# Self-attention's row maxima turned by VectorE and two DMAs instead of by TensorE and ScalarE, from the fourth batch on

## What is computed

```python
q = qkv[:, :, 0].transpose(0, 2, 1, 3)
k = qkv[:, :, 1].transpose(0, 2, 1, 3)
v = qkv[:, :, 2].transpose(0, 2, 1, 3)
attn = jnp.einsum('bhnd,bhsd->bhns', q, k) * SCALE
attn = jax.nn.softmax(attn, axis=-1)
o = jnp.einsum('bhns,bhsd->bhnd', attn, v)
```

## Time and profile before

| | us |
|---|---|
| median of 3 runs | 2573.73 |
| lowest and highest | 2573.45, 2574.57 |
| the profiled execution | 2577.71 |
| its span, first instruction to last | 2575.9 |
| what lies around the span | 1.8 |

### The profile page before, as it was taken

How to read it: one execution, slowest core, us unless ns; L and a number is a source line. 1 busy time by engine, 2 the same in 40 slices (tenths; PEclk the granted TensorE clock), 3 DMA queues, 4 the chain that set the end, 5 groups by cost and what they waited for, 6 DMA issues and landing times.

```text
span 2575.9 us, 66165 instructions
## 1 busy us (share of the span) xinstructions
PE 2479.3 (96%) x27466; PEld 1848.3 (72%) x27466; DVE 1858.5 (72%) x3532; ACT 1274.0 (49%) x1810; POOL 467.2 (18%) x510
## 2 busy tenths in 40 slices
PE   5779999999999999999999999999999999999998
PEld 3557777777777777777777777777777777777767
DVE  4767777777777777777777767777677677776752
ACT  1345544555555555555455554554555545445443
POOL 0111211212111211111121211211212212112121
PEclk7889999999999999999999999999999999999999
DMA  5322222222222223232122122132231222222211
GB/s 188 129 93 78 78 74 74 74 80 87 83 77 76 90 81 96 77 101 68 56 76 74 56 76 74 62 96 78 80 107 60 82 84 78 78 66 80 82 33 42
DMA packets 236749, 207.56 MB, mean 81 GB/s; under 512 B 87682, under 2 KB 222020, under 8 KB 236452
## 3 DMA queue, kind: packets, MB, share of 16 engines
q1 hardware_dynamic: 236452, 203.32, 24.7%
HBM read 58.34 MB, written 4.39 MB: 24 GB/s over the span
## 4 chain that ended last, share of the span: by engine, by line
PE 79%; DVE 12%; issue 3%; ACT 3%; SPq 2%; DMA 1%; POOL 1%; DVEq 0%; POOLq 0%; ACTq 0%
PE o_acc L1340 11%; PE score L1287 10%; PE ring L1371 10%; PE ring L1248 10%; PE ring L1362 10%; PE score L1309 8%; PE ring L1352 6%; DVE row_max_F L978 5%; DVE row_max_G L978 5%; PE ring L1144 4%; PE ring L1256 3%; PE score L1314 3%; PE ring L1268 2%; ACT probs L1117 2%; PE ring L1271 2%
## 5 line engine op out<-in xcount | busy, mean ns | idle before, releaser
L1117 ACT ACTIVATE probs<-score 120x2048 f32<-120x2048 f32 (+1 forms) x320 | 601.6, 1880 | 374.8 <-PE score L1314 368.0
L978 DVE TENSOR_REDUCE row_max_F<-score 128x8 f32<-128x2048 f32 x192 | 438.7, 2285 | 103.3 <-PE score L1287 102.8
L1371 PE MATMUL ring<-w_fc,h_t 128*128 128x256 f32 x1536 | 368.9, 386 | 1.0 <-ACT h_t L1128 1.0
L1362 PE MATMUL ring<-x_t_E,w_fc 128*128 128x256 f32 x1536 | 368.3, 386 | 0.0
L978 DVE TENSOR_REDUCE row_max_G<-score 128x16 f32<-128x1920 f32 x128 | 276.1, 2157 | 116.8 <-PE score L1287 116.8
L1128 ACT ACTIVATE h_t<-ring,cols 128x256 f32<-128x256 f32 x384 | 160.7, 470 | 341.1 <-PE ring L1362 341.0
L1362 PEld LDWEIGHTS ring<-x_t_E,w_fc 128*128 128x128 f32 x1536 | 280.8, 190 | 59.3 <-issue 20.3
L1000 DVE STREAM_TRANSPOSE o_turned<-o_acc 128x512 f32<-128x512 f32 x224 | 159.9, 714 | 220.3 <-PE o_acc L1340 220.3
L1371 PEld LDWEIGHTS ring<-w_fc,h_t 128*128 128x128 f32 x1536 | 282.5, 190 | 46.3 <-ACT h_t L1128 1.4
L1340 PE MATMUL o_acc<-probs,v_self 128*17 128x256 f32 x3072 | 204.3, 384 | 0.0
L793 POOL TENSOR_TENSOR x<-x,gated 128x256 f32<-128x256 f32 x96 | 70.3, 733 | 723.1 <-DVE gated L1032 723.1
(11 more groups left out here) (136 smaller groups left out, 3770.9 us busy)
## 6 DMA issues: line engine op xcount, KB each, us to landing
q_G<-q_parts SPq DMA_DIRECT2D x256, 128.0 KB, 2.1
q_F<-q_parts SPq DMA_DIRECT2D x192, 128.0 KB, 2.1
k_F<-k_parts SPq DMA_DIRECT2D x96, 256.0 KB, 2.5
k_F<-k_parts SPq DMA_DIRECT2D x192, 128.0 KB, 2.2
k_G<-k_parts SPq DMA_DIRECT2D x128, 120.0 KB, 2.2
k_G<-k_parts SPq DMA_DIRECT2D x256, 60.0 KB, 1.9
gate_now_P<-gate_rows SPq DMA_DIRECT2D x48, 256.0 KB, 3.2
gate_now_E<-gate_rows SPq DMA_DIRECT2D x48, 256.0 KB, 3.4
```

What stands on the lines that cost most here:

```text
L978: nc.vector.tensor_reduce(dst, src, AX.X, ALU.max).then_inc(row_max_ready[r].sem, 1)
L1117: nc.scalar.activation(probs[v % 2][0:keys, :, :], score[0:keys, :].rearrange("p (h q) -> p h q", h=2 * GROUPS), ACT.Exp, scale=SCALE).the ...
L1362: last = mm(ps[:, c % 2 * NT:(c % 2 + 1) * NT], w_fc1[:, k, c * P:(c + 1) * P], buffer(x_t, r, m, n)[:, k, :], start=k == 0, stop=k == KC - 1)
L1371: last = mm(ps[:, 0:D], h_t[:, k, t * P:(t + 1) * P], w_fc2[:, k, :], start=k == 0, stop=k == MC - 1)
```

## The change

For the first three self-attention jobs nothing changes, nor for any of cross-attention. For the other 45 the change does this:

- `X`: DVE packs the 16 x 2 parts of each query into the first 32 columns of `max_parts_F` and then transposes these in squares of 32x32 (one instruction, 128 partitions x 64 columns) into the new `max_turned_F`. It waits for its own last instruction before that.
- `X` on SP: when that is done, a DMA writes `max_turned_F` to a DRAM tensor `max_rows_F` of 32 rows of 256: pieces of 128 bytes, 256 of them (32 KB).
- `M` on SP: when that has landed, a DMA reads the 32 rows four times, once for each group of 32 partitions, into `max_t_F` (128 rows of 1 KB, 128 KB).
- `M` on PE and ACT falls away: no transposes, no buffer of the ring, no copy.
- `T0` on PE waits for the second DMA instead of for ACT. The product that adds the maxima takes a second selection, `sel_moved`, which DVE makes once at the start of the program from five more small instructions.

```diff
+def by_transfers(r, m, n, nb):
+    return r == "F" and FULL_BEFORE[m] * nb + n >= 3
...
-        if step in RING_STEPS:
+        if step in RING_STEPS and not (step == "M" and by_transfers(r, m, n, nb)):
             here = at % RING
             at += 1
...
+        max_rows = {r: nc.dram_tensor(f"max_rows_{r}", [32, NT], F32, kind="Internal").ap() for r in "FG"}
...
+                if step == "X" and by_transfers(r, m, n, nb):
+                    sp.wait_ge(max_turned_ready[r].sem, max_turned_ready[r].after(m, n))
+                    if moved_order[r][m, n] > 0:
+                        sp.wait_ge(max_laid[r].sem(m, n), max_laid[r].after(m, n) - 16)
+
+                    sp.dma_start(max_rows[r].rearrange("h (t a q) -> a h t q", t=TT, a=4), max_turned[r][:, :, :])\
+                        .then_inc(max_written[r].sem(m, n), 16)
+                elif step == "M" and by_transfers(r, m, n, nb):
+                    sp.wait_ge(max_written[r].sem(m, n), max_written[r].after(m, n))
+                    t_psum[r].wait_before(sp, m, n)
+                    sp.dma_start(max_t[r][:, :], max_rows[r].unsqueeze(0).to_broadcast([GROUPS, 32, NT]))\
+                        .then_inc(max_laid[r].sem(m, n), 16)
...
+            for g in range(GROUPS):
+                at = slice(32 * g, 32 * (g + 1))
+                last = nc.vector.tensor_reduce(pair_rows_moved[at, :], ident[at, 40 * g:40 * g + 2 * PAIRS]
+                                               .rearrange("p (c e) -> p c e", e=2), AX.X, ALU.add)
+            last.then_inc(pair_rows_ready, 1)
+            dve.wait_ge(pair_rows_ready, 2)
+            nc.vector.tensor_copy(sel_moved[:, :].bitcast(F32R), pair_rows_moved[:, :]).then_inc(sel_ready, 1)
...
                     src = row_max[r][:, :, :, :].rearrange("p t g c -> p (t g) c")
+                    if by_transfers(r, m, n, nb):
+                        src = row_max[r][:, :, :, :].rearrange("p t g c -> p t (g c)")
...
+                    if by_transfers(r, m, n, nb):
+                        parts = max_parts[r][:, :, 0:32].rearrange("p t (b e) -> p t b e", e=2)
...
+                    if by_transfers(r, m, n, nb):
+                        dve.wait_ge(max_parts_ready[r].sem, max_parts_ready[r].after(m, n))
+                        if moved_order[r][m, n] > 0:
+                            dve.wait_ge(max_written[r].sem(m, n), max_written[r].after(m, n) - 16)
+                        nc.vector.transpose(max_turned[r][:, :, :],
+                                            max_parts[r][:, :, 0:32])\
+                            .then_inc(max_turned_ready[r].sem, 1)
...
-                elif step == "M":
+                elif step == "M" and not by_transfers(r, m, n, nb):
                     act.wait_ge(m_psum[r].sem, m_psum[r].after(m, n))
                     t_psum[r].wait_before(act, m, n)
...
-                elif step == "M":
+                elif step == "M" and not by_transfers(r, m, n, nb):
                     pe.wait_ge(max_parts_ready[r].sem, max_parts_ready[r].after(m, n))
...
                     if v == 0:
-                        pe.wait_ge(max_t_ready[r].sem, max_t_ready[r].after(m, n))
+                        if by_transfers(r, m, n, nb):
+                            pe.wait_ge(max_laid[r].sem(m, n), max_laid[r].after(m, n))
+                        else:
+                            pe.wait_ge(max_t_ready[r].sem, max_t_ready[r].after(m, n))
...
+                    selection = sel_moved if by_transfers(r, m, n, nb) else sel
```

More of the change, by code:

```diff
@@ L270, in build_program @@
     cross_order = {job: i for i, job in enumerate(cross_jobs)}
+    max_moved = {r: [job for job in jobs if by_transfers(r, *job, nb)]
+                 for r, jobs in (("F", list(self_order)), ("G", cross_jobs))}
+    max_made = {r: [job for job in jobs if not by_transfers(r, *job, nb)]
+                for r, jobs in (("F", list(self_order)), ("G", cross_jobs))}
     normed_order = {job: i for i, job in enumerate(job for job in cross_jobs if CTX_LN[job[0]])}
@@ L289, in build_program @@
         sel = sb("sel", [P, PAIRS])
+        pair_rows_moved = sb("pair_rows_moved", [P, PAIRS])
+        sel_moved = sb("sel_moved", [P, PAIRS])
         minus_half = sb("minus_half", [P, TT])
@@ L345, in build_program @@
         max_parts = {r: sb(f"max_parts_{r}", [P, TT, P]) for r in "FG"}
+        max_turned = {r: sb(f"max_turned_{r}", [P, TT, 32]) for r in "F"}
         max_t = {r: sb(f"max_t_{r}", [P, NT]) for r in "FG"}
@@ L382, in build_program @@
         s_psum = signals("s_psum", "FG", {"F": 4, "G": 2})
-        m_psum = signals("m_psum", "FG")
+        m_psum = {r: Signal(semaphore(f"m_psum_{r}"), 1, {job: i for i, job in enumerate(max_made[r])}) for r in "FG"}
         t_psum = signals("t_psum", "FG", {"F": 4, "G": 2})
@@ L394, in build_program @@
         k_high_ready = signals("k_high_ready", "FG")
-        max_t_ready = signals("max_t_ready", "FG")
+        max_t_ready = {r: Signal(semaphore(f"max_t_ready_{r}"), 1, m_psum[r].order) for r in "FG"}
         probs_ready = signals("probs_ready", "FG", {"F": 4, "G": 2})
@@ L409, in build_program @@
         max_parts_ready = signals("max_parts_ready", "FG")
+        moved_order = {r: {job: i for i, job in enumerate(max_moved[r])} for r in "FG"}
+        max_turned_ready = {r: Signal(semaphore(f"max_turned_ready_{r}"), 1, moved_order[r]) for r in "FG"}
         o_turned_ready = signals("o_turned_ready", "FG", 2)
@@ L429, in build_program @@
         k_laid = semaphore("k_laid")
+        max_written = {r: Turns([semaphore(f"max_written_{r}")], moved_order[r]) for r in "FG"}
+        max_laid = {r: Turns([semaphore(f"max_laid_{r}")], moved_order[r]) for r in "FG"}
         x_stored = semaphore("x_stored")
@@ L1314, in _ @@
                             last = mm(score[0:keys, g * BANK + e * NT:g * BANK + (e + 1) * NT],
[L1315 removed]
+                                      selection[at, 2 * c + e:2 * c + e + 1].bitcast(F32R).to_broadcast([32, keys]),
                                       max_t[r][at, :].bitcast(F32R),
```

8 lines of the change are left out of this document (6 added, 2 removed).

## The result

| | before | changed |
|---|---|---|
| median of 16 runs each, in turn on one chip | 2573.89 | 2581.53 |
| lowest and highest | 2571.86, 2579.32 | 2577.24, 2586.68 |
| the profiled execution | 2577.71 | 2583.16 |
| its span | 2575.9 | 2581.3 |

The ratio is 1.0026, with a 95% interval of 1.0019 to 1.0033: **slower by 7.6 us**. That is more than the 5.1 us (0.2%) that the prediction took as the least that can be told from no change, so the forecast of no change was wrong, though 2581.5 lies in its range. The profiled executions differ by 5.4.

What follows compares the result with a forecast made beforehand. DVE's maximum, not PE, was taken to set the next step's start in 41 of 45 turns. All terms were 0 except -0.7 us in the last job's turn: 2577.0 profiled, 2573.0 for the median, range 2571 to 2585.

Steps and rivals of the forecast that it cites:

- The shadow: In 41 of 45 turns, DVE's maximum of G sets when `G.S1` starts, so removing PE's transposes there wins 0 us.
- rival 2: PE's time comes back: all 45 x 0.42 = 19 us are won, giving 2555; chance 0.06.
- The four turns left: Turns 3 to 5: up to 1.3 us, taken as 0; last job's turn: 0.7 us won at `F.T0`.
- DVE's transpose: Square transpose ahead of `G.S0`'s maximum: 0.24 us, maximum not moved, 0.11 us to spare; 0 us taken.
- Rival 3: DVE's spare 0.11 us is not enough: `G.S0`'s maximum slips 0.1 in 25 turns, +2.5 us, 2576; chance 0.14, counted with "same".
- any cost at the start: Five more small DVE instructions at program start, 1.4 us, fit into DVE's 4.67 us of idle time: 0 us.
- The write: SP's DMA of the maxima to DRAM, issued behind the gate load: 3.0 us taken, bounds 2.1 and 4.0.
- The read: DMA from DRAM into `max_t_F`: 3.2 us taken, bounds 2.1 and 4.1; both DMAs done 0.3 us ahead of `F.T0`'s need.
- The rival's ground: By the cited rule, a leading broadcast of 4 confines a DMA to 4 engines, so both new DMAs run on 4.
- rival 1: Both DMAs late on 4 engines: `F.T0` 1.7 us late, 0.7 left behind `F.T3`, 25 x 0.7 = 17 us, 2590; chance 0.20.
- What a late `F.T0` would cost: In TURN turns PE's 1.05 us wait at `F.T3` swallows the delay: 0 us taken, 14 us with all upper bounds.
- The first step of the same prediction: Reading the timeline around `F.M` in all 45 turns for what ends last: DVE's maximum in 41; 0 us won there.

Runs made afterwards that it cites:

- write_twice: Changed kernel with one more DMA ahead of each write of the maxima, the same 32 KB into a spare DRAM tensor: 2606.12 us, ratio 1.0114.

## Why the prediction failed

*The shadow: right.* `G.S1` follows the maximum's end by 0.05 us as before, and comes 3.44 us behind `G.S0` in all 41 turns of the kernel before and in 40 of the changed one (3.54 in the turn of job 37). PEld is idle 0.43 in the TURN turn shown, where it was 0.25, and 0.81 in the WITH_L1 turn, where it was 0.43. The row of after for that turn:

```profile
619.58 0.97 PEld L1342 LDWEIGHTS score<-k_G,q_G 32*128 32x128 f32 x32 [0.81 <-DVE row_max_G L1017]
```

I had expected 0.65 in TURN turns, because I took the transposes at their busy time, 0.42. PE's timeline, two rows of before and one of after, shows less:

```profile
1515.26 0.44 PE L1144 MATMUL ring<-ident,max_parts_F 128*128 128x128 f32 x2
1515.54 1.89 PE L1352 MATMUL ring<-w_cp,o_t_B 128*128 128x256 f32 x8
...
1516.62 1.99 PE L1411 MATMUL ring<-w_cp,o_t_B 128*128 128x256 f32 x8
```

From the transposes' start to the start of `B.PR` it is 0.28 us, since matmuls overlap; and `B.PR`, now directly behind `G.S0`, takes 1.99 instead of 1.89, its first matmul 483 ns instead of 382. So 0.18 us leaves PE in such a turn, which is the growth of the idle time (0.43 less 0.25). With 0.38 in a WITH_L1 turn that is 10.6 us for the 41 turns, not 17 (PE's busy sum, whose ends are modelled, fell by 7), and rival 2's price of 19 us was too high for the same reason. Rival 2 (faster) is out: without the lateness the ratio is 0.9995.

*The four turns left: roughly right.* The turns of jobs 4 and 5 are 0.2 us shorter each, where I took 0 with a bound of 0.42. The last job's turn, forecast at 0.7, is 0.75 shorter in the kernel with the gate load behind.

*DVE's transpose: right.* 0.245 us by 45 instructions, predicted 0.24; 0.15 to spare, predicted 0.11. In one turn of 25, job 37's, the maximum did start 0.1 late. Rival 3 is out. So is any cost at the start: DVE is idle for 4.11 us there, against 4.67.

*The write: right.* Blocked on SP behind the gate load, as worked out, and 2.87 us to land, predicted 3.0.

*The read: mis-sized.* 3.2 was taken, from the gate rows, as "spread in the same manner"; they are spread with a leading dimension of 128, this read with 4, so it was not the same. 3.8 was measured, inside the bounds (2.1 to 4.1); single reads came to 4.2 in TURN turns and 4.9 in WITH_L1 turns. The rival's ground, 4 engines, is confirmed by the increments, by the packets, and by the four separate reads, which land in 3.0. I had the rule and gave it 0.20 since the values could absorb it; the trace of before had no DMA of that form to weigh it by. That the quickest reads land in 3.2, as taken, is luck, since the row used is of another form and twice the size; and what puts the median at 3.8 is mostly packets that are held, which the sum did not have. The usual pair takes 2.99 + 3.8, and `F.T0` starts 0.13 behind the landing: 6.9 us against 6.6, 0.3 late, and it was held in 17 of 26 jobs. That is between my forecast (0.3 early) and rival 1 (1.7 late).

*What a late `F.T0` would cost: **this step failed**.* "Later in the same turn PE waits for ACT's exponential at `F.T3`, 1.05 us [...] A delay of PE up to 1.05 us is swallowed there." That was one turn, the one I had opened. The first step of the same prediction was looked at in all 45 turns, this one was not; in 19 of 25 turns there is no such wait, and in 23 it is under 0.3. Without the swallowing the same sum gives another answer: 0 at the values taken, but 1.6 a turn, 40 us, at the upper bounds, and 0.3 a turn, 8 us, with the read at 3.8. That is near the measured 7.6 us. It took both errors: the read at 3.8 with a delay of up to 1.05 swallowed in each turn would have cost nothing, and so would no swallowing with the read at 3.2. Two runs settle it: write_twice, where 23.5 us more of waiting made the stretch of the late jobs 22.4 longer, and the gate load moved behind, which takes the waits and the whole loss away. Rival 1's condition, more than 7.9 us for the pair, was wrong for the same reason: without the 1.05 it needed only 6.8, about what the pair took.

## What to carry to other kernels

A slack that is to swallow a delay must be shown in every turn in which the delay can come; the idle time of the group, summed over the program (5.7 us for 48 jobs), tells at once whether one turn speaks for all. A step that leaves the busiest engine is worth only what it was worth at its place: here it stood in the shadow of another engine, and its removal gave no time back, that of its sister step 0.1 us a turn. What it takes there is read from start to start, not from its busy time (0.18 us against 0.42 here). When a short path on the chip is replaced by a DMA chain, put its issue ahead of every load that doesn't hurry, and look at how both sides of the DMA divide among the queues' engines before a landing time is borrowed from a DMA of another form.

## What the runs showed of the hardware

- A read of 128 KB from DRAM, spread with a leading dimension of 4, had 5 semaphore increments, about four packets under way at a time (a DMA share of 0.25), and landed in 3.2 to 4.9 us (the changed kernel); cut into four DMAs of 32 KB with 16 increments each it landed in 3.0 from the first issue where SP did not pause, 1.7 us for each; q's copies of 128 KB inside SBUF take 2.1.
- A packet of 1 KB of that read took 46 ns, one of 128 bytes of the write 13 ns. In 16 of 26 reads, three or more packets took 0.2 to 1.0 us; the cause is open.
- PE started 0.13 us after the last increment of the DMA that it waited for.
- A write of 32 KB into DRAM in 256 pieces of 128 bytes landed in 2.35 us with nothing ahead of it, in 2.87 behind a load of 256 KB issued 0.45 us earlier. The slowing was 0.5 us for that one load, and a further write of the same size ahead cost 0.9 us a turn.
- SP took 0.56 to 0.62 us to issue either of the two DMAs in the changed kernel, 0.33 to 0.43 for the gate load; and in nine turns 0.7 to 1.5 us longer for four reads in a row, for a reason that stays open.
- A square transpose on DVE of 128 x 64 float32 took 245 ns, on the line through 256 and 512 columns (445 and 714).
